# TensorE's blocks without a loop, two steps of attention moved into the block before, and w2 loaded later

## The chip, the cores and the metric

The kernel runs on one core of one Trainium2 chip. The metric is the device time in microseconds (us) of one execution; three runs of the kernel before are given, and one profiled execution. In the profile PE is TensorE's matmuls, PEld its weight loads, DVE VectorE, ACT ScalarE, POOL GpSimd and SP the engine that issues most DMAs; a q behind a name (SPq) is that engine's instruction queue.

## What is computed

A layer of a vision transformer over 32 images of 3 x 96 x 96, cut to 36 patches each: 1152 tokens of width 192. The token step, one attention layer with 12 heads of 64, and one layer of 8 experts of which each token uses one:

```python
out = jnp.einsum('rbnp,rep->bne', y, W_proj) + b_proj.sum(axis=0)      # tokens h
qkv = layernorm(h) @ W_qkv.T
logits = jnp.einsum('bhtd,bhsd->bhts', q, k) / SCALE                   # SCALE = 1/8
att = jax.nn.softmax(logits, axis=-1)
h = h + cat(att @ v) @ W_out.T
expert_idx = jnp.argmax(softmax(xt @ gate_w + gate_b), axis=-1)        # xt = layernorm(h)
for e in range(8):                                                     # gelu exact
    y = gelu(xt @ w1[e] + b1[e]) @ w2[e] + b2[e]
    out = jnp.where((expert_idx == e)[:, None], y, out)
h = h + out
```

## The kernel before, in words

The tokens are worked in NB = 4 blocks of BT = 288 tokens, each of NT = 3 row tiles of 96 tokens, and for attention in NU = 4 groups of two images (72 tokens). Each engine has its own program; semaphores join them. An opening does block 0's tokens, heads and values and the first scores. Then `body(b)` runs four times on TensorE, ScalarE, VectorE and GpSimd: three times in a hardware loop (`Fori(0, NB - 1)`, lines 670, 888, 1171, 1319) and once, shorter, for the last block (`last`). Since block b + 1's heads and values are computed in body b, a body holds: block b's attention, block b + 1's tokens, block b's output projection, norm and gate, and then block b + 1's q, k, v and scores 0 to 2. After the last body the tokens are ranked and gathered by expert and 16 tiles of 128 tokens run through the experts.

Attention of a group g takes these steps: `scores(g)` (TensorE, L465), `soften(g)` (VectorE, L994 and L995: subtract the maximum, frees the scores' banks by `sc_free`), `exponentials(g)` (ScalarE, L802), `normalise(g)` (VectorE, L1003 to L1005), `turn_probs(g)` (TensorE, L480, a transpose by 24 small matmuls, traced as 48), `take_probs(g)` (ScalarE, L816), `attend(g)` (TensorE, L495, product with v), `take_attended(g)` (ScalarE, L822). `turn_probs(g)` waits for the `take_probs` of the group before; `attend(g)` in the first place waits for `sc_free` of soften(3), since it writes the scores' banks.

Products into the four accumulator banks go through `product(key, b)`: the position of a key in `MIDDLE` (or `OPENING`, `FINAL`) modulo 4 gives its bank, so a product waits (`into`) until the one four keys before it has been taken out. In `MIDDLE` the keys from 6 are o0, o1, QK[0], QK[1], gt0, QK[2], o2, QK[3], QK[4], gt1, QK[5], QK[6], QK[7], gt2: ("o", 2) is number 12 and QK[5] number 16.

Around the row tiles: `project(t)` (TensorE, L506) gives a row tile of the attention's output, `take_o(t)` (VectorE, L1080) adds the residual, frees the bank and takes the statistics, `inverse_std` (GpSimd, L1290 and L1293) gives the inverse root, `finish_row(t)` (VectorE, L952) the normed row, `turn_rows(t)` (TensorE, L426) its transpose.

In each of the three loop bodies a third of w1 is split for the experts: `round_w1(b, 1)` on ScalarE (L786) copies w1B_part, `split_w1(b, 2)` and `split_w1(b, 3)` on VectorE (L1017) wait for it, `round_w1(b, 2)` (L788) copies the rest. In the body `split_w1(b, 2)` stands behind `take_o(2)` and `split_w1(b, 3)` last, behind `rank_tokens`.

SP's queue issues, in order: the first loads, the x of the following blocks, the normed rows of a block to the table in DRAM (`send_rows`), and for the last part w2 (4608 KB, into the memory of w_qkv, behind the last product with v of block 2's body), the rows of block 2, b2, half of b1 when the last attend is done (into the memory of v), the last rows, the other half of b1. TensorE waits for w2 (`w2_here`) before the experts, VectorE for b2 before `take_x` and for b1 before `add_b1`. GpSimd gathers the token rows from the table when all rows are sent and `ids` is there.

## Time and profile before

| | us |
|---|---|
| median of 3 runs | 319.29 |
| the runs | 319.29, 323.86, 317.44 |
| profiled execution | 320.99 |
| its span | 319.2 |
| PE / PEld busy | 270.7 / 246.5 |
| DVE / ACT / POOL busy | 171.2 / 130.1 / 64.1 |
| mean granted clock of TensorE | 0.918 |

The span is the time from the first to the last instruction; the rest of the profiled execution's 320.99 lies around it. Busy times of PE are those of pipelined matmuls. The program moves 28.12 MB at a mean of 88 GB/s. By the chain of work that ended last, TensorE holds 70% of the span, VectorE 11%, time in which an engine waited for nothing that the profile shows ("issue") 10%, ScalarE 5%.

### The profile page before, as it was taken

What the parts mean: (1) busy time and instruction counts of PE and PEld (TensorE: products, weight loads), DVE (VectorE), ACT (ScalarE), POOL (GpSimd) and SP (SyncE); (2) the same over time, 40 slices, a digit from 0 to 9 for tenths busy, and PEclk for the clock granted to TensorE, in tenths of its full rate; (3) what the DMA queues carried; (4) which work ended last, traced back from release to release, by engine and by line L of the source; (5) the groups of instructions that cost most, each with busy time, mean ns of one, the idle gap of its engine ahead of it and who ended that gap; (6) DMA issues with size and microseconds to landing.
All of it is one profiled execution on the core that took longest, in us unless ns stands there. A gap on an engine that the chain in (4) does not pass through costs nothing.

```text
span 319.2 us, 9680 instructions
## 1 busy us (share of the span) xinstructions
PE 270.7 (85%) x3710; PEld 246.5 (77%) x3711; DVE 171.2 (54%) x491; ACT 130.1 (41%) x354; POOL 64.1 (20%) x102
## 2 busy tenths in 40 slices
PE   7948989998999989499989747867479999999981
PEld 7928879897889987389988646747459998988871
DVE  7974286443787536836535840137146755655530
ACT  3463545535458364535454621220025344344220
POOL 2540002031003310002310000010602334334221
PEclk9987999799999999869999955695899999999997
DMA  7988600301001110000000393645300222121100
GB/s 258 267 321 326 265 3 4 113 3 55 3 0 28 83 55 0 6 4 2 4 0 2 113 422 118 191 149 212 99 26 13 63 74 49 55 68 34 31 3 0
DMA packets 6174, 28.12 MB, mean 88 GB/s; under 512 B 1495, under 2 KB 2787, under 8 KB 4990
## 3 DMA queue, kind: packets, MB, share of 16 engines
q1 hardware_dynamic: 4350, 23.62, 20.9%
q0 software_dynamic: 1792, 4.04, 4.7%
q8 instruction: 25, 0.41, 0.5%
q14 instruction: 7, 0.06, 0.1%
HBM read 24.99 MB, written 3.34 MB: 89 GB/s over the span
## 4 chain that ended last, share of the span: by engine, by line
PE 70%; DVE 11%; issue 10%; ACT 5%; POOL 1%; DVEq 1%; POOLq 0%; ACTq 0%
PE psum L433 22%; PE psum L714 10%; PE psum L506 9%; PE psum L418 5%; PE psum L480 4%; PE psum L495 4%; PE psum L542 4%; PE psum L702 3%; ACT w1B_part L786 2%; DVE total L1003 2%; PE psum L465 2%; PE psum L566 1%; DVE top L994 1%; DVE kT L995 1%; PE psum L426 1%
## 5 line engine op out<-in xcount | busy, mean ns | idle before, releaser
L1290 POOL TENSOR_SCALAR veps<-mv 96x1 f32<-96x1 f32 x24 | 8.2, 341 | 164.3 <-DVE mv L948 164.1
L433 PE MATMUL psum<-xn_hi,wq_parts 128*128 128x288 f32 x144 | 36.1, 320 | 4.0 <-DVE late_r L968 2.9
L714 PE MATMUL psum<-w2s,kT 128*128 x192 | 34.7, 331 | 2.8 <-issue 1.4
L714 PEld LDWEIGHTS psum<-w2s,kT 128*128 128x128 f32 x192 | 30.8, 190 | 4.8 <-issue 4.7
L506 PE MATMUL psum<-wo,oT 128*96 128x192 f32 x144 | 31.0, 376 | 0.7 <-ACT oT L822 0.7
L480 PE MATMUL psum<-ident,kT 36*36 36x36 f32 x768 | 18.8, 209 | 12.8 <-issue 7.7
L433 PEld LDWEIGHTS psum<-xn_hi,wq_parts 128*128 128x128 f32 x144 | 25.6, 197 | 5.0 <-issue 3.2
L480 PEld LDWEIGHTS psum<-ident,kT 36*36 36x36 f32 x768 | 16.8, 125 | 16.1 <-issue 15.3
L506 PEld LDWEIGHTS psum<-wo,oT 128*96 128x96 f32 x144 | 27.0, 193 | 2.3 <-issue 0.9
L433 PE MATMUL psum<-wq_parts,xn_hi 128*100 128x384 f32 x96 | 28.4, 350 | 0.0
L433 PE MATMUL psum<-late_r,wq_parts 128*128 128x288 f32 x96 | 28.4, 303 | 0.0
L1341 POOL DMA_INDIRECT out<-oT,ids x16 | 16.1, 1007 | 53.4 <-DVE oT L1229 53.4
L908 ACT ACTIVATE qT<-qT 128x512 f32<-128x512 f32 (+1 forms) x32 | 15.0, 515 | 25.3 <-DVE qT L1215 25.3
L433 PE MATMUL psum<-wq_parts,late_r 128*100 128x384 f32 x64 | 21.4, 335 | 0.0
L810 ACT COPY late<-psum 100x384 f32<-100x384 f32 x32 | 14.9, 476 | 15.8 <-PE psum L433 15.8
L1215 DVE TENSOR_TENSOR qT<-psum,late 128x512 f32<-128x512 f32 (+1 forms) x32 | 16.4, 553 | 8.3 <-PE psum L433 8.3
L418 PE MATMUL psum<-late,xb 128*96 128x192 f32 x108 | 20.0, 341 | 0.0
L1204 DVE TENSOR_TENSOR fx_lo<-psum,xn_hi 128x128 fp32r<-128x128 f32 x16 | 4.7, 292 | 27.4 <-issue 16.5
L1330 POOL DMA_INDIRECT xb<-token_table,ids x16 | 15.8, 985 | 16.9 <-DVE ids L1193 11.8
L433 PEld LDWEIGHTS psum<-late_r,wq_parts 128*128 128x128 f32 x96 | 18.9, 197 | 0.0
L418 PEld LDWEIGHTS psum<-late,xb 128*96 128x96 f32 x108 | 17.8, 170 | 0.5
L495 PE MATMUL psum<-late 36*64 36x36 f32 x768 | 17.4, 238 | 0.5 <-issue 0.4
(151 smaller groups left out, 573.2 us busy)
## 6 DMA issues: line engine op xcount, KB each, us to landing
w2s<-w SPq DMA_DIRECT2D x1, 4608.0 KB, 14.7
xb<-xT SPq DMA_DIRECT2D x4, 864.0 KB, 4.8
w1A_in<-w SPq DMA_DIRECT2D x3, 1024.0 KB, 7.5
w1B_in<-w SPq DMA_DIRECT2D x3, 1024.0 KB, 9.6
late<-b SPq DMA_DIRECT2D x2, 1536.0 KB, 7.4
token_table<-rows SPq DMA_DIRECT2D x4, 432.0 KB, 4.0
late<-w_proj SPq DMA_DIRECT2D x1, 960.0 KB, 4.9
kT<-b SPq DMA_DIRECT2D x1, 768.0 KB, 4.1
```

The source lines that it names most:

```text
L418: mm = pe.matmul(dst[0:TT, 0:D], xb[:, k, t * TT:(t + 1) * TT], weff[:, k // 2, k % 2, :], start=(k == 0), stop=(k == KX - 1))
L433: mm = pe.matmul(dst, lhsT, rhs, start=(i == 0), stop=(i == len(parts) - 1))
L480: mm = pe.matmul(psum[image, TR_BANK, cols], probs[image, g, cols], ident[image, image], start=True, stop=True)
L495: mm = pe.matmul(psum[DH * k:DH * (k + 1), SIDE_BANKS[i], at:at + PER_IMAGE], v[image, g, col:col + DH], probsT[image, g % 2, j * PER_IMAG ...
L506: mm = pe.matmul(dst[0:TT, 0:D], oT[:, c, t * TT:(t + 1) * TT], wo[:, c, :], start=(c == 0), stop=(c == PAIRS - 1))
L542: pe.transpose(psum[:, bank, 0:P], ident[:, :], ident[:, :])
L714: mm = pe.matmul(psum[:, 6, 0:D], hidT[i % 2][:, c * P:(c + 1) * P], w2s[:, bass.ds(e, 1), c, :], start=(c == 0), stop=(c == FCH - 1))
L810: act.copy(v[0:SPAN, g, f * (HD // 2):(f + 1) * (HD // 2)], acc(slot[0])[0:SPAN, 0:HD // 2]).then_inc(free[slot[0]], 1)
L908: ge = act.activation(hid[i % 2][:, lo:hi], hid[i % 2][:, lo:hi], ACT.Gelu)
L1215: dve.tensor_tensor(hid[i % 2][:, lo:hi], psum[:, 2 * (i % 2) + k, 0:hi - lo], b1s[:, bass.ds(e, 1), lo:hi].rearrange("p o f -> p (o f)"), ...
L1330: pool.indirect_dma_start(out=xg[j % 4], out_offset=None, in_=table, in_offset=bass.IndirectOffsetOnAxis(ap=ids[:, j:j + 1], axis=0)).then ...
L1341: pool.indirect_dma_start(out=out, out_offset=bass.IndirectOffsetOnAxis(ap=ids[:, j:j + 1], axis=0), in_=yo[j % 4], in_offset=None, bounds ...
```

## The change

TensorE's three bodies are written out, with a Python loop in place of `Fori`; the other engines keep theirs. The semaphore increments `passed("pe", pe)` go. `turn_probs(0)` and `scores(3)` of a block, which stood at its body's head, now stand in the tail of the body before (or of the opening), on TensorE around `ranks`; with them go `take_probs(0)` and `exponentials(3)` on ScalarE and `normalise(2)` and `soften(3)` on VectorE. `normalise(3)` becomes the first step of VectorE's body. `split_w1(b, 2)` moves ahead of `take_o(2)` and `split_w1(b, 3)` behind it, ahead of `finish_row(2)`. On SP's queue w2, b2 and the whole of b1 are issued one after another when the last attend is done; the rows of the last block are sent from ScalarE's queue, between `take_rows(1)` and `take_rows(2)`.

```diff
@@ sync
-                if b == NB - 2:
-                    complete(sp, product(VALUES[-1], b))
-                    sp.dma_start(w2s[:, :, :, :], w2).then_inc(w2_here, 16)
                 send_rows(b)
-            sp.wait_ge(tr_full, NU * NB)
+            sp.wait_ge(av_full, NU * NB)
+            sp.dma_start(w2s[:, :, :, :], w2).then_inc(w2_here, 16)
             sp.dma_start(b2s, b2.partition_broadcast(P)).then_inc(b2_here, 16)
-
-            sp.wait_ge(av_full, NU * NB)
-            sp.dma_start(b1s[:, 0:EXPERTS // 2, :], b1[0:EXPERTS // 2].partition_broadcast(P)).then_inc(b1_here, 16)
-            send_rows(NB - 1)
-            sp.dma_start(b1s[:, EXPERTS // 2:, :], b1[EXPERTS // 2:].partition_broadcast(P)).then_inc(b1_here, 16)
+            sp.dma_start(b1s, b1.partition_broadcast(P)).then_inc(b1_here, 16)
@@ tensor: scores, turn_probs and attend each lose passed("pe", pe); then the opening
-                if n in (0, 2, 4):
+                if n in (0, 2, 4, 7):
                     if n == 0:
                         all_taken(pe, QK, 0, opening=True)
-                    scores(n // 2, 0)
+                    scores({0: 0, 2: 1, 4: 2, 7: 3}[n], 0)
+                if n == 6:
+                    turn_probs(0, 0)
@@ tensor: body
-                attend_first()
                 if last:
+                    turn_probs(1, b)
                     pe.wait_ge(sc_free, NU * b + 5)
-                    attend_next(0)
+                    attend(0, b)
                     attend_next(1)
...
                 tokens(1, product(("tok", 1), b))
+                turn_probs(1, b)
                 pe.wait_ge(sc_free, NU * b + 5)
-                attend_next(0)
+                attend(0, b)
...
                 next_values((2, 1), (3, 0))
+                turn_probs(0, b + 1)
                 ranks(b)
                 next_values((3, 1))
+                scores(3, b + 1)
...
-            with pe.Fori(0, NB - 1) as b:
+            for b in range(NB - 1):
                 body(b, False)
@@ scalar
+            take_probs(0, 0)
+            exponentials(3, 0)
...
-                take_probs(0, b)
-                exponentials(3, b)
...
                     take_rows(1)
+                    act.wait_ge(rows_ready, NT * b + NT + 1)
+                    act.dma_start(table[b * BT:(b + 1) * BT, :].rearrange("(t p) d -> p t d", p=TT),
+                                  rows[:, :, :]).then_inc(rows_sent, 16)
                     take_rows(2)
...
-                next_values((3, 0), (3, 1))
+                next_values((3, 0))
+                take_probs(0, b + 1)
+                next_values((3, 1))
+                exponentials(3, b + 1)
                 round_w1(b, 2)
@@ vector
-            for g in range(3):
+            for g in range(NU):
                 soften(g, 0)
-                if g < 2:
+                if g < NU - 1:
                     normalise(g, 0)
...
-                normalise(2, b)
-                soften(3, b)
+                normalise(3, b)
                 if last:
-                    normalise(3, b)
...
                 take_tokens(0, product(("tok", 0), b))
-                normalise(3, b)
                 take_tokens(1, product(("tok", 1), b))
...
                 finish_row(1)
+                split_w1(b, 2)
                 take_o(2)
-                split_w1(b, 2)
+                split_w1(b, 3)
                 finish_row(2)
...
                 soften(2, b + 1)
+                normalise(2, b + 1)
+                soften(3, b + 1)
                 rank_tokens()
-                split_w1(b, 3)
...
-            dve.wait_ge(b1_here, 32)
+            dve.wait_ge(b1_here, 16)
```

## Rows read from the trace of the kernel before

**Rows 1.** Windows cut at TensorE's blocks 0, 1, 2 and the last attention.

```profile
core 0: us, PE busy (x) PEld busy (x) DVE busy (x) ACT busy (x) POOL busy (x), PEclk, DMA share, GB/s
45.13:88.91 43.78, 42.04 (x783) 38.44 (x782) 24.53 (x78) 21.89 (x62) 6.33 (x13) 0.96 0.10 33
88.91:131.16 42.25, 40.24 (x782) 36.94 (x781) 27.20 (x87) 23.41 (x63) 6.33 (x13) 1.00 0.10 32
131.16:180.15 48.99, 42.43 (x783) 38.85 (x782) 27.25 (x87) 23.55 (x63) 6.33 (x13) 0.93 0.01 3
180.15:195.50 15.35, 7.56 (x290) 7.16 (x289) 6.69 (x17) 5.74 (x9) 0.00 (x0) 0.66 0.87 338
```

**Rows 2.** Timeline of TensorE, head of block 2 (start, us, ..., idle before).

```profile
133.21 0.23 PE L480 MATMUL psum<-ident,kT 36*36 36x36 f32 x2 [2.05 <-issue]
136.47 1.48 PE L480 MATMUL psum<-ident,kT 36*36 36x36 f32 x43 [3.03 <-issue]
...
138.71 5.11 PE L418 MATMUL psum<-late,xb 128*96 128x192 f32 x24
```

**Rows 3.** DMA queue of instructions (packets, MB, share): block 1, then block 2.

```profile
q8 instruction: 2, 0.03, 0.4%
...
q8 instruction: 8, 0.13, 1.2%
```

**Rows 4.** Timelines of PE, ACT, DVE, POOL in the middle of block 1.

```profile
113.44 0.38 PE L433 MATMUL psum<-xn_hi,wq_parts 128*128 128x288 f32 x1
...
115.40 0.40 PE L433 MATMUL psum<-xn_hi,wq_parts 128*128 128x288 f32 x1 [0.38 <-ACT qT L792]
...
116.83 0.27 PE L426 MATMUL psum<-ident,rows 96*128 96x96 f32 x1 [0.50 <-DVE rows L952]
...
113.15 1.90 ACT L786 CAST w1B_part<-w1B_in 64x2048 fp32r x1
...
112.18 0.35 DVE L1080 TENSOR_TENSOR rows<-psum,hres 96x192 f32<-96x192 f32 x1 [1.23 <-PE psum L506]
...
115.17 1.22 DVE L1017 TENSOR_TENSOR w1B<-w1B_in,w1B_part 64x1024 f32 x1 [1.92 <-ACT w1B_part L786]
...
113.75 0.56 POOL L1293 TENSOR_TENSOR rstd<-veps,minus_half 96x1 f32<-96x1 f32 x1
```

**Rows 5.** Timeline of TensorE, turn 1 near the head of block 1.

```profile
95.12 0.96 PE L480 MATMUL psum<-ident,kT 36*36 36x36 f32 x45 [0.66 <-DVE kT L995]
```

**Rows 6.** Timelines: a projection in block 1; the last attention; ScalarE there.

```profile
102.93 2.12 PE L506 MATMUL psum<-wo,oT 128*96 128x192 f32 x12
...
181.00 0.87 PE L465 MATMUL psum<-kT,qT 64*36 64x36 f32 x46
186.26 1.56 PE L480 MATMUL psum<-ident,kT 36*36 36x36 f32 x45 [4.39 <-DVE kT L995]
...
192.65 0.76 PE L480 MATMUL psum<-ident,kT 36*36 36x36 f32 x18 [2.65 <-issue]
...
195.50 3.76 PE L506 MATMUL psum<-wo,oT 128*96 128x192 f32 x12 [0.74 <-ACT oT L822]
...
180.86 1.90 ACT L788 CAST w1B<-w1B_in  x1
```

**Rows 7.** An issue of SP; DMA issues (KB each, median us to landing); stores of rows (min/median/max).

```profile
204.09 0.33 SPq L402 DMA_DIRECT2D late<-b  x1
...
w2s<-w SPq DMA_DIRECT2D x1, 4608.0 KB, 14.7
late<-b SPq DMA_DIRECT2D x2, 1536.0 KB, 7.4
xb<-token_table,ids POOLq DMA_INDIRECT x16, 3.2
...
DMA to landing us min/median/max: 3.2/4.0/15.5
```

**Rows 8.** Timelines of GpSimd and VectorE: first gather, first product with b1 added.

```profile
224.55 1.24 POOL L1330 DMA_INDIRECT xb<-token_table,ids  x1 [11.80 <-DVE ids L1193]
...
235.15 1.02 DVE L1215 TENSOR_TENSOR qT<-psum,late 128x512 f32<-128x512 f32 x2
```

More of the change, by code:

```diff
@@ L283, in build @@
         pool_step = sem("pool_step")
-        waited = {"pe": sem("pe_waited"), "dve": sem("dve_waited"), "pool": sem("pool_waited")}
+        waited = {"dve": sem("dve_waited"), "pool": sem("pool_waited")}
         ident_ready = sem("ident_ready")
@@ L458, in scores @@
                 pe.wait_ge(sc_free, NU * b + g + 1)
-                passed("pe", pe)
                 for c in range(PAIRS):
@@ L474, in turn_probs @@
                 pe.wait_ge(tr_free, NU * b + g + 1)
-                passed("pe", pe)
                 for j in range(HEADS):
@@ L487, in attend @@
                 pe.wait_ge(av_free, NU * b + g + 1)
-                passed("pe", pe)
                 for c in range(PAIRS):
@@ L600, in products @@
                         heads(*key, product(key, b))
-                def attend_first():
-                    turn_probs(0, b)
-                    scores(3, b)
                 def attend_next(g):
```

## The prediction

> **What bounds the kernel now.** I read the windows first, cut at the starts of TensorE's blocks. In the first three blocks TensorE is busy for 42.04 of 43.78, 40.24 of 42.25 and 42.43 of 48.99 us [rows 1]: there TensorE is the path, and only its waits can be won. The reader is to see that blocks 0, 1 and 2 issue the same 782 or 783 matmuls and that block 2 is 48.99 − 42.25 = 6.74 us longer than block 1. Then the last attention: from 180.15 to 195.5 TensorE is busy for only 7.56 of 15.35 us at a granted clock of 0.66 [rows 1]. The timeline of TensorE says where: two stalls of 2.05 and 3.03 us at the head of block 2, released by nothing the profile shows [rows 2]; a wait of 4.39 us in the last block and, with w2 in flight, another stall of 2.65 us without a releaser [rows 6]. Last I read which instruction-queue packets ran: 2 in block 1, 8 in block 2 [rows 3].
>
> **The change, part by part.** Sums are in us against the profiled execution (span 319.2 in a run of 320.99); that run is 1.7 above the median of 319.29, and I carry the difference over to the median.
>
> *Loop written out (D).* Block 1 fetched almost nothing: its code was there from block 0. Block 2 fetched 8 packets and stood for 5.1 us at its first turn [rows 2, 3]; the rest of its 6.74 is the slow clock after it. Straight code reads on without a jump, so block 2 should cost what block 1 costs: −6.74. The price of no loop is that blocks 1 and 2 fetch all their code (E). Block 0 did so in straight order and took 43.78 at clock 0.96 against block 1's 42.25 at 1.00, a difference of 1.53 [rows 1]. Low end 0, high end 1.53 for block 1 and as much for block 2 again, 3.1. Block 2 after its stall streamed without another stall, so I take 0.5.
> The Trainium skill (Runtime: NRT & Kernel Launch, Instruction fetch mechanics) says that prefetch is purely sequential, that crossing a block of code is mostly hidden, and that a taken branch out of the resident window stalls. The trace agrees for the second jump (5.1 us) and not for the first, which shows no stall. By the page E would be 0 and the total 0.5 lower.
>
> *Turn 0 and scores 3 in the tail (C).* The same instructions run in almost the same order, so TensorE's own work is worth 0. What goes is the wait for soften(3) ahead of turn 1 in a middle block, 0.66 [rows 5]. But normalise(3) now stands ahead of take_tokens(0) on VectorE, behind rank_tokens, so the statistics of token tile 0 come about 1 us later and turn_tokens(0) waits for them. I take half: −0.3 at two boundaries, −0.6 (ends −1.3 and +0.6).
>
> *split_w1 moved around take_o(2) (A, B).* This part costs. In block 1, take_o(2) ran at 112.18. The product that begins at 113.44 (QK[5]) writes the accumulator bank that o2 used: key 12 and key 16 of MIDDLE, four banks. It therefore waits for take_o(2). Now split_w1(b, 2) stands ahead of take_o(2), and this split waits for ScalarE's w1B_part, a copy from 113.15 to 115.05: the split runs from 115.17 for 1.22 us [rows 4]. take_o(2) then starts at 116.31 and ends at 116.66, QK[5] starts at about 116.8 instead of 113.44: TensorE stands 3.3 us. Next late: the third row. From the start of take_o(2) to the end of its inverse root were 114.31 − 112.18 = 2.1 us [rows 4], now to 118.4; split 3 (1.22) behind the statistics ends at 118.6; finish_row(2) gives its transpose at about 119.0, against 116.83. QK[5] to QK[7] end at 118.8, so the end of this place moves by 119.0 − 116.83 = 2.15; the old waits of 0.38 and 0.50 are in it. Three blocks: +6.45 (A). The clock: after a gap of 5.1 us TensorE came back slow, twenty-four token matmuls after it included [rows 2]; after small waits it did not. A gap of 3.3 lies between. If the clock falls, QK[5] to QK[7] (2.05) take twice as long, less the 0.2 of slack, and what follows loses a little: 0 to 2 a block. I take 0.7, +2.1 for three (B). What split 3 gives back behind rank_tokens (1.22 on VectorE) is already in C. The twelve semaphore increments that go from TensorE's queue in each block I cost at 0: queued matmuls hide them; all the idle time of block 1 is 42.25 − 40.24 = 2.0 us [rows 1], and the waits named here (0.66, 0.38, 0.50) fill most of it.
>
> *The last attention (F).* Before, scores(3) ends at 181.87 and project(0) starts at 195.50, 13.6 later [rows 6]. Now soften(3) is done about 1.4 after scores(3); turn 1 fills the time; attend(0) ends at 2.2. Turn 2 needs take_probs(1), which is queued on ScalarE behind exponentials(3) (to 2.0) and round_w1(b, 2) (1.90 [rows 6]), so it ends at 4.4. Then turn 2 and attend(1) (0.9 + 0.8), copy out of attended (0.6), project(0) at 6.9; at half clock 7.7. Win 6.7 or 5.9; if the clock stays full, project(0) takes 2.12 instead of 3.76 [rows 6] and the win is 8.3. The stall of 2.65 beside w2 is inside this: w2 no longer flies then. I take −6.2 (ends −8.3 and −5.3). From project(0) on the chain of projections, norms, gate and ranks is as before.
>
> *w2, b2 and b1 behind the last attend; rows on ScalarE's queue (G).* Call A the end of the last attend (204.0 before, where SP issued the first half of b1 [rows 7]). w2 took 14.7 to land, half of b1 7.4 [rows 7]. In series, w2 at A+14.8, b2 (half the bytes of that b1 half, 3 to 4) at about A+18, b1 whole at A+26 to A+33 by these latencies, and at A+25 if they pipeline at w2's rate (4.7 MB in 14.7 us against 8.65 MB). TensorE needs w2 at about A+20; the first gather leaves at A+20.5, VectorE needs b1 at 235.15, A+31.2 [rows 8]. So w2 is covered by 5 us, b1 by 6 when pipelined, by nothing if serial at 33 (+2). But the first gathers now run beside b1, and TensorE waits for the first: 3.2 alone [rows 7]. The last rows are stored at A+9, now beside w2: such a store took 3.2 to 15.5 to land, the 15.5 queued behind w2 [rows 7]; landing at A+24.5 would hold the gathers by 4. Range 0 to 4.3; nearest row is the gather itself, half as long again: I take +1.5. The issue on ScalarE (about 0.3, as SP's) hides under TensorE's transpose of the third row. rows(2) no longer queue behind w2; nobody waited for them.
> The Trainium skill (DMA: Bandwidth & Descriptors, Queues, rings and completion order) says that a DMA engine takes turns packet by packet between the queue rows with work, and that SP and ScalarE own a row each. By that the last rows would not stand behind w2 and G is at its low end; by a single line it would be 4.3. No row of this trace has two such queues loaded.
>
> **Sum.** A 6.45 + B 2.1 + C −0.6 + D −6.74 + E 0.5 + F −6.2 + G 1.5 = −3.0. 319.3 − 3.0 = **316.3 us**, 0.9% less. About 2% (6.4 us) is what a measurement of this kernel can tell from no change: the three runs shown lie 317.44 to 323.86. So: no difference that counts.
>
> **Rivals.**
> 1. *The clock holds.* B = 0, project(0) at full clock (F −8.3), fetch free, G half: 6.45 − 0.6 − 6.74 − 8.3 + 0.7 = −8.5, **310.8**. For it: 0.66 and 0.38 of idle left the clock up. Against: the last attention keeps gaps of over 2 us and ran at 0.66. Chance 0.24.
> 2. *The gathers start late.* G = 4.3, rest as forecast: **319.1**. For it: 8.65 MB behind one another until A+25. Against: separate queues. Chance 0.12.
> 3. *Slower: straight code is fetched late.* Place: heads of code blocks while x or rows move, in blocks 1 and 2. Price of one late fetch: 2.65 as beside w2 [rows 6] and 1.7 of slow clock, 4.35. Three of them give −3.0 − 0.5 + 13.05 = +9.6, **328.9**; over 2% slower from the third on. For it: TensorE's two kinds of unexplained stall both came with fetches. Against: block 0 and the rest of block 2 streamed with at most 1.53 lost. Chance 0.07.
> 4. *The change does not do what it says:* the stall at block 2's head is no matter of the loop and returns. D = 0: **323.0**. For it: the first jump had no stall. Against: 8 packets against 2. Chance 0.07.
> Forecast: 0.50, its own range 313 to 320.
>
> **How the numbers follow.** Faster by over 2% (under 312.9): four fifths of rival 1 and 0.04 of the forecast, 0.23. Slower (over 325.7): rival 3 and a little of 4, 0.09. Within: 0.68. Range 310.5 to 322: it leaves out rival 3, half of rival 4 and the far end of rival 1.
>
> **What would show it.** D: no gap over 1 us at a block's head, block 2 within 1.5 of block 1. A: a wait of about 3.3 us of a QK product on VectorE's take_o(2) in each of three blocks, and turn_rows(2) waiting for finish_row(2). B: granted clock below 1.00 behind it. C: the 0.66 gone, perhaps a wait of turn_tokens(0). F: project(0) of the last block 7 to 8 us behind scores(3). G: first gather over 3.2 us, no wait of TensorE on w2. The forecast is wrong if QK[5] does not wait (then −9 or more), if w2 or b1 lands after its need, or if fetch stalls spread.

## The result, and the profile after

| | before | after |
|---|---|---|
| median, us | 318.49 (4 runs) | 327.07 (4 runs) |
| all runs, us | 317.44, 317.68, 319.29, 323.86 | 326.83, 326.88, 327.27, 330.33 |
| span of the profiled execution, us | 319.2 | 325.1 |
| granted clock of TensorE | 0.918 | 0.91 |

Some executions of this kernel fall in a slower state; all ratios leave them out, while the medians are over all executions. The ratio is 1.0305, with a 95% interval of 1.0215 to 1.0395: slower by 3%, where 316.3 us and "no difference that counts" were forecast. 327.07 lies 5 us above the upper end of the range, 322.

The page of the changed kernel, part 5 (group | busy, mean ns | idle before, what ended most of it) and part 4 (shares of the chain that ended last), already shows two of the causes:

```profile
PE 69%; DVE 9%; issue 6%; DMA 6%; ACT 5%; POOL 2%; DVEq 1%; POOLq 0%; ACTq 0%
...
L427 PE MATMUL psum<-xn_hi,wq_parts 128*128 128x288 f32 x144 | 40.1, 347 | 12.0 <-DVE rows L1078 9.2
...
L1327 POOL DMA_INDIRECT xb<-token_table,ids x16 | 15.7, 984 | 22.5 <-DMA token_table<-rows 17.1
```

The products with q and k now wait 9.2 us in all for `take_o` (L1078), three times 3.06. The gathers wait for the store of the last rows, and 6% of the chain is a DMA; before, the first gather followed `ids` on VectorE [rows 8].

To find where the time went, I cut both traces at the same four events of TensorE: the start of each block's token products, the end of the last block's fourth scores, and the start of its first output projection. Windows of after, then the same cuts in before (columns as in [rows 1]):

```profile
core 0: us, PE busy (x) PEld busy (x) DVE busy (x) ACT busy (x) POOL busy (x), PEclk, DMA share, GB/s
46.47:94.00 47.53, 43.55 (x788) 39.80 (x782) 25.49 (x75) 22.52 (x63) 7.17 (x13) 0.93 0.10 31
94.00:144.80 50.80, 46.20 (x788) 41.94 (x782) 27.41 (x86) 23.70 (x63) 7.16 (x13) 0.87 0.09 28
144.80:190.74 45.94, 41.72 (x796) 38.32 (x792) 27.40 (x86) 23.52 (x63) 7.17 (x13) 0.96 0.04 12
190.74:198.88 8.14, 4.72 (x193) 4.41 (x188) 4.78 (x17) 4.43 (x6) 0.00 (x0) 0.76 0.01 2
```

```profile
46.55:90.32 43.77, 42.03 (x787) 38.43 (x781) 24.68 (x81) 22.18 (x62) 6.33 (x13) 0.96 0.10 33
90.32:138.71 48.39, 41.30 (x789) 37.89 (x781) 30.18 (x93) 25.05 (x64) 6.33 (x13) 0.95 0.09 29
138.71:181.87 43.16, 41.66 (x784) 38.03 (x781) 24.51 (x80) 22.23 (x61) 6.33 (x13) 0.98 0.05 13
181.87:195.50 13.63, 5.85 (x193) 5.67 (x193) 5.37 (x11) 4.04 (x7) 0.00 (x0) 0.62 0.86 348
```

The three blocks are 3.8, 2.4 and 2.8 us longer, although the second no longer holds the loop's stall of 5.1 us [rows 2]. The last attention is 5.5 us shorter, a little less than the 5.9 to 6.7 of the forecast.

Each of the three blocks holds this place. Timelines of TensorE, VectorE and GpSimd in block 0 of after, and windows around it:

```profile
71.09 0.25 PE L420 MATMUL psum<-ident,rows 96*128 96x96 f32 x1
71.17 0.24 PE L421 MATMUL psum<-ident,rows 96*64 96x96 f32 x1
74.48 0.40 PE L427 MATMUL psum<-xn_hi,wq_parts 128*128 128x288 f32 x1 [3.06 <-DVE rows L1078]
...
76.05 0.44 PE L427 MATMUL psum<-late_r,wq_parts 128*128 128x288 f32 x1
...
72.94 1.22 DVE L1015 TENSOR_TENSOR w1B<-w1B_in,w1B_part 64x1024 f32 x1 [4.22 <-ACT w1B_part L778]
74.08 0.34 DVE L1078 TENSOR_TENSOR rows<-psum,hres 96x192 f32<-96x192 f32 x1
...
75.08 1.22 DVE L1015 TENSOR_TENSOR w1B<-w1B_in,w1B_part 64x1024 f32 x1
...
75.34 1.04 POOL L1287 TENSOR_SCALAR veps<-mv 96x1 f32<-96x1 f32 x1 [7.04 <-DVE mv L946]
```

```profile
73.00:75.50 2.50, 1.02 (x7) 1.02 (x8) 2.32 (x5) 0.42 (x4) 0.16 (x1) 0.99 0.00 0
75.50:78.50 3.00, 3.00 (x15) 2.78 (x14) 1.17 (x2) 1.47 (x5) 2.10 (x3) 0.50 0.05 16
```

VectorE is idle for 4.22 us in front of the split, which waits for ScalarE's copy of w1B_part; `take_o(2)` stands behind it, and TensorE's QK[5] behind that. After the gap the granted clock is 0.50 for 3 us, the lower of the two levels (1.2 of 2.4 GHz), and a product takes 0.44 instead of 0.30 us. In blocks 1 and 2 the same wait of 3.06 stands at 124.36 and 171.43.

At the other end, the last store and the first gather. Issues of ScalarE's queue and of GpSimd, TensorE's wait, and the DMA issues of 203 to 236 us (KB each, us to landing):

```profile
213.66 0.35 ACTq L854 DMA_DIRECT2D token_table<-rows  x1
...
230.36 1.24 POOL L1327 DMA_INDIRECT xb<-token_table,ids  x1 [17.14 <-DMA token_table<-rows]
...
w2s<-w SPq DMA_DIRECT2D x1, 4608.0 KB, 14.3
late<-b SPq DMA_DIRECT2D x1, 3072.0 KB, 22.9
kT<-b SPq DMA_DIRECT2D x1, 768.0 KB, 16.3
token_table<-rows ACTq DMA_DIRECT2D x1, 432.0 KB, 15.8
```

A store of 432 KB that had a queue to itself took 15.8 us, as long as the slowest store before, which stood behind w2 on one queue (15.5 [rows 7]). The first gather left at 230.36 instead of 224.55 [rows 8].

### The profile page after: what moved, and what is told of

Its sections match the earlier page's. It is cut to its first block, busy times and chain, and to the rows that moved or that the text cites. A ratio compares the mean times of both kernels' runs of the same rounds, so it can differ in the third digit from the quotient of the medians.

```text
span 325.1 us, 9601 instructions
## 1 busy us (share of the span) xinstructions
PE 273.1 (84%) x3710; PEld 247.9 (76%) x3711; DVE 171.5 (53%) x491; ACT 130.5 (40%) x354; POOL 66.6 (20%) x102
## 3 DMA queue, kind: packets, MB, share of 16 engines
q0 software_dynamic: 1792, 4.04, 4.5%
## 4 chain that ended last, share of the span: by engine, by line
PE 69%; DVE 9%; issue 6%; DMA 6%; ACT 5%; POOL 2%; DVEq 1%; POOLq 0%; ACTq 0%
PE psum L427 27%; PE psum L706 10%; PE psum L497 8%; DMA token_table<-rows 5%; PE psum L472 4%; PE psum L486 3%; PE psum L694 3%; PE psum L458 2%; PE psum L533 2%; PE psum L412 2%; ACT w1B_part L778 2%; PE psum L557 1%; DVE top L992 1%; DVE total L1001 1%; PE psum L420 1%
## 5 line engine op out<-in xcount | busy, mean ns | idle before, releaser
L427 PE MATMUL psum<-xn_hi,wq_parts 128*128 128x288 f32 x144 | 40.1, 347 | 12.0 <-DVE rows L1078 9.2
L1287 POOL TENSOR_SCALAR veps<-mv 96x1 f32<-96x1 f32 x24 | 10.7, 446 | 168.1 <-DVE mv L946 167.5
L427 PEld LDWEIGHTS psum<-xn_hi,wq_parts 128*128 128x128 f32 x144 | 29.1, 224 | 13.0 <-DVE rows L1078 9.8
L427 PE MATMUL psum<-late_r,wq_parts 128*128 128x288 f32 x96 | 31.1, 330 | 0.0
L497 PE MATMUL psum<-wo,oT 128*96 128x192 f32 x144 | 30.0, 366 | 0.7 <-ACT oT L814 0.7
L497 PEld LDWEIGHTS psum<-wo,oT 128*96 128x96 f32 x144 | 26.0, 187 | 2.0 <-issue 0.8
L1338 POOL DMA_INDIRECT out<-oT,ids x16 | 16.1, 1007 | 53.3 <-DVE oT L1226 53.3
L427 PEld LDWEIGHTS psum<-late_r,wq_parts 128*128 128x128 f32 x96 | 21.5, 224 | 0.0
L472 PEld LDWEIGHTS psum<-ident,kT 36*36 36x36 f32 x768 | 15.6, 120 | 5.7 <-issue 4.9
L472 PE MATMUL psum<-ident,kT 36*36 36x36 f32 x768 | 17.5, 204 | 2.6 <-ACT late L808 2.2
L784 ACT COPY qT<-psum 128x288 f32<-128x288 f32 x24 | 9.5, 398 | 23.0 <-PE psum L427 23.0
```

The lines of the kernel that those rows point to most:

```text
L427: mm = pe.matmul(dst, lhsT, rhs, start=(i == 0), stop=(i == len(parts) - 1))
L472: mm = pe.matmul(psum[image, TR_BANK, cols], probs[image, g, cols], ident[image, image], start=True, stop=True)
L497: mm = pe.matmul(dst[0:TT, 0:D], oT[:, c, t * TT:(t + 1) * TT], wo[:, c, :], start=(c == 0), stop=(c == PAIRS - 1))
L1287: pool.tensor_scalar(veps[:, kind, t:t + 1], mv[:, kind, t, 1:2], EPS, None, ALU.add).then_inc(pool_step, 1)
L1338: pool.indirect_dma_start(out=out, out_offset=bass.IndirectOffsetOnAxis(ap=ids[:, j:j + 1], axis=0), in_=yo[j % 4], in_offset=None, bounds ...
```

## The experiments

Each ratio is that to the kernel before, run on the same chip in the same batch.

### 1. The order of split_w1, undone and alone

```diff
# undo_split: the changed kernel with
+                take_o(2)
                 split_w1(b, 2)
-                take_o(2)
-                split_w1(b, 3)
                 finish_row(2)
...
                 rank_tokens()
+                split_w1(b, 3)
# split_only: the kernel before with the opposite edit
```

> The changed kernel, with split_w1(b, 2) and split_w1(b, 3) where they stood before (behind take_o(2), and behind rank_tokens). Theory: each of three blocks loses about 3.5 us because QK[5] waits for take_o(2), 2.2 of wait and 1.3 of slow clock behind it; so 327.1 - 10.5 = about 316.6 us, and no wait of TensorE on line L1078. Rival 1, the wait is covered by other work or taken back in the tail: 325 to 327. Rival 2, only the wait counts and the clock falls anyway: 320.5.

> The kernel before, with split_w1(b, 2) ahead of take_o(2) and split_w1(b, 3) ahead of finish_row(2), and nothing else changed. Theory: TensorE waits about 3.1 us for take_o(2) in each of three blocks and is slow behind it, +3.5 a block, about +10: 329. Rival, it costs only beside the other parts: under +4.

`undo_split`: 319.01 us, ratio 0.9956 (0.9908 to 1.0003), span 319.1. By the ratios that is 3.5% or 11 us under the changed kernel; the two medians, from different batches, are 8 us apart. Its block 0 took 43.90 against 47.53 us, 3.63 less, and around QK[5] only the two old waits of 0.38 and 0.49 us stand. From the start of block 0 to the end of the last scores(3) it took 181.31 − 46.47 = 134.84 against 144.27 us, 9.4 less. `split_only`: 332.44 us, ratio 1.0293 (1.0171 to 1.0414), with the wait of 3.06 us at 73.48, 129.90 and 175.82. Its ratio rests on two executions, and its trace also holds 1.4 us more of stalls without a releaser, up to the end of the last attention, than that of the kernel before, so not all of its 2.9% need be the order's. From both sides the order costs about 3%; this one part is as large as the whole loss.

### 2. The third row ahead of the second half of the split

```diff
                 take_o(2)
-                split_w1(b, 3)
                 finish_row(2)
+                split_w1(b, 3)
```

> The changed kernel with finish_row(2) ahead of split_w1(b, 3) instead of behind it. In the changed kernel GpSimd's first step of the third row took 1.04 us instead of 0.22 beside that split. Theory (the wait of 3.06 us of QK[5] for take_o(2) and the slow clock behind it are the whole cost, the third row is ready while TensorE still works through the slowed products): GpSimd's step is 0.22 again, the wait of 3.06 stays, the block's length stays within 0.3 us, 326 to 327 us. Rival (the third row sets the end of this place, as the sum of the prediction had it): 0.8 to 2 us less in each of three blocks, 321 to 324.5.

328.88 us, ratio 1.0145 (1.0084 to 1.0205), span 328.7. The interval doesn't meet that of the changed kernel, but the spans and the trace don't show this kernel to be faster: block 0 took 94.23 − 46.70 = 47.53 us, as in the changed kernel, the three blocks together 190.91 − 46.70 = 144.21 against 144.27, and the wait of 3.06 is there in each. The expected time (326 to 327) was missed by 2 us; another batch and another chip stand behind this one, with 323.76 for the kernel before. GpSimd's step, timeline of block 0:

```profile
75.65 0.22 POOL L1287 TENSOR_SCALAR veps<-mv 96x1 f32<-96x1 f32 x1 [7.03 <-DVE mv L946]
75.95 0.56 POOL L1290 TENSOR_TENSOR rstd<-veps,minus_half 96x1 f32<-96x1 f32 x1
77.10 1.49 POOL L1313 COPY hres<-h 96x576 f32<-96x576 f32 x1 [0.58 <-DVE rows L950]
```

So the step of 1.04 us is back at 0.22, and TensorE gains nothing: it is still busy with products at the lower clock when the row is ready. The product's own wait and the clock behind it are the cost, not the third row.

### 3. The loads and the last store, undone and alone

```diff
# undo_dma: the changed kernel with SP's queue of before (w2 from the last
# product with v of block 2 on, ahead of that block's rows; half of b1, the
# last rows, the other half); no store from ScalarE.
# undo_both: this and undo_split. dma_only: the kernel before with
+            sp.wait_ge(av_full, NU * NB)
+            sp.dma_start(w2s[:, :, :, :], w2).then_inc(w2_here, 16)
...
+                    act.dma_start(table[...], rows[:, :, :]).then_inc(rows_sent, 16)
```

> The changed kernel, with the loads of w2, b2 and b1 and the store of the last rows as before (w2 behind block 2's last product with v, rows on SP's queue between the halves of b1). Theory: the first gather no longer waits for the store of the last rows, -5.3 us; against that a stall of TensorE beside w2 in the last attention comes back, 2.65 us and slow clock, +0 to +5: 322 to 327. Rival, the late gather came from something else: it stays 5 us behind ids, 327 and more.

> The changed kernel with both the split order and the loads as before; what is left is TensorE without a loop and turn 0 and scores 3 in the tail. Theory: the two are independent and add: 327.1 - 10.5 - 5.3 + (0 to 5) = 311 to 316 us. If they do not add, the clock ties them together.

> The kernel before, with the loads of w2, b2 and b1 behind the last attend and the last rows stored from ScalarE's queue, nothing else changed. Theory: the store lands 15 us after its issue and the gathers wait 4 to 5 us for it; against that the stall of 2.65 beside w2 in the last attention goes, with some slow clock: +1 to +3, 320 to 322. Rival, the store is no slower than before: 315 to 316.

`undo_dma`: 329.33 us, ratio 1.0281 (1.0154 to 1.0409), span 329.2. `undo_both`: 318.97, 0.9937 (0.9882 to 0.9993), span 315.7. `dma_only`: 326.32, 1.016 (1.0075 to 1.0246), span 321.9. With the store of before, the gathers follow `ids` at once; but nothing is seen to be won, since a wait comes up elsewhere. VectorE in the last block of `undo_both`, then TensorE behind it:

```profile
187.27 0.61 DVE L1006 TENSOR_TENSOR kT<-kT,share 100x432 f32<-100x432 f32 x1
197.49 0.35 DVE L1081 TENSOR_TENSOR rows<-psum,hres 96x192 f32<-96x192 f32 x1 [9.61 <-DMA token_table<-rows]
...
200.18 0.39 PE L426 MATMUL psum<-ident,rows 96*128 96x96 f32 x1 [3.93 <-DVE rows L953]
```

`take_o(0)` of the last block overwrites the rows of block 2, whose store stands behind w2 on SP's queue. In the kernel before the last attention took 13.6 us and `take_o(0)` ran at 199.39, released by its projection; the store was out in time. Now that the attention takes 8.1, the store is late (in `undo_dma` the wait is 11.29, and 6.15 on TensorE). "Nobody waited for them", said the prediction; that held for before only. The stall of 2.65 us beside w2 was expected back here and didn't come: in `undo_dma`, `undo_both` and `rows_first` (experiment 8) w2 is in flight during the last attention and no such stall stands there, while `loop_back` has one of 2.10 us there with nothing of w2 in flight. So w2 was not its cause. And `dma_only` prices the changed DMA part by itself: its store took 16.1, its first gather left 17.44 us after GpSimd's last step, TensorE waited 7.27 us for it.

### 4. w2 and b1 in eight DMAs each

```diff
-            sp.dma_start(w2s[:, :, :, :], w2).then_inc(w2_here, 16)
+            for e in range(EXPERTS):
+                sp.dma_start(w2s[:, e:e + 1, :, :], w2[:, e:e + 1]).then_inc(w2_here, 16)
# b1 likewise; the waits count to 16 * EXPERTS
```

> The changed kernel, with w2 and b1 loaded in eight DMAs each (one expert each) at the same place and in the same order; the bytes are the same, a packet is an eighth (36 KB and 24 KB of one partition in one packet become 4.6 and 3 KB). Theory 1, a DMA engine takes turns between SP's and ScalarE's queues packet by packet: 19 packets of rows per engine stand each behind one large packet; with small ones the store lands in 4 to 6 us, not 15.8, and the time is 327.1 - 5.3 = about 321.8. Theory 2, a store waits for all bytes issued earlier, whatever the packets: it lands after 14 to 16 us and the time stays 327.

325.2 us, ratio 1.0183 (1.0091 to 1.0274), span 322.1. The last store landed after 8.6 instead of 15.8 us (the expectation said 4 to 6), and the gathers left at 225.20, right behind `ids`. Not all of that is won: now b1 is loaded beside the first gather, and from its issue to TensorE's first product 5.26 us pass instead of 3.36. 321.8 us had been expected. What a packet is, and who gets turns, the queues' rows show (packets, MB, share of 16 engines): in the changed kernel from 214 to 216 us, 218 to 220, 220 to 222, 224 to 226, then in `pieces` from 220 to 222.

```profile
q1 hardware_dynamic: 22, 0.81, 94.1%
...
q1 hardware_dynamic: 53, 0.63, 75.2%
q10 hardware_dynamic: 54, 0.08, 11.0%
...
q1 hardware_dynamic: 109, 0.68, 82.1%
q10 hardware_dynamic: 115, 0.18, 23.4%
...
q1 hardware_dynamic: 34, 0.84, 96.9%
q10 hardware_dynamic: 34, 0.05, 6.9%
```

```profile
q1 hardware_dynamic: 185, 0.56, 70.8%
q10 hardware_dynamic: 153, 0.21, 28.5%
```

q1 is SP's queue, q10 ScalarE's, which holds nothing but the 304 packets of the rows (0.44 MB, 1.4 KB each). It has no packet in the first 2 us, nor has it one in the first 3 us behind the issue in `pieces`. After that the counts of the two run side by side, 53 to 54, 109 to 115, 34 to 34: one turn each. But a packet of w2 is 0.81 MB / 22 = 37 KB, one of b1 0.84 / 34 = 25 KB, one of b2 6 KB. Beside b1 the rows get 7% of the engines, in the stretch where w2 ends and b2 begins 11%; beside b2 they get 23%, beside the smaller pieces 28%. The Trainium skill (DMA: Bandwidth & Descriptors, Queues, rings and completion order) says that a DMA engine takes turns packet by packet between queue rows, and the counts agree. It was my conclusion from it, "G is at its low end", that fell: a fair turn is no fair share when the packets differ eighteen to twenty-five fold.

### 5. The loop: written out alone, and put back

```diff
# unroll_only: the kernel before with
-            with pe.Fori(0, NB - 1) as b:
-                body(b, False)
+            for b in range(NB - 1):
+                body(b, False)
# loop_back: the changed kernel with the opposite edit and the passed("pe") of before
```

> The kernel before, with TensorE's three bodies written out and nothing else changed. Theory of the prediction: the 5.1 us at the head of block 2 go and the clock stays up behind it, -6.7; against it blocks 1 and 2 fetch their code, and beside the load of x in block 1 TensorE is late once and slows, as in block 0: +0 to +4. So 312 to 316 us where the kernel before takes 318.5. Rival, the stall is not the loop's: 318.5 and a gap at a block's head.

> The changed kernel with TensorE's loop back (and its semaphore increments at the waits); all else as changed. Theory: a stall of 3 to 5 us at the head of a block comes back, with slow clock behind it, and the late fetch of block 1 goes: +0 to +6 against the changed kernel. Rival, written out or not is the same to TensorE: within 1 us and a gap at the same place.

`unroll_only`: 315.78 us, ratio 0.986 (0.9788 to 0.9932), span 314.7. The stall at the head of block 2 is gone, as forecast, but not all of its 6.7 us is won: from the start of block 0 to the end of the last scores(3) it took 179.19 − 46.27 = 132.92 against 135.32 us before, 2.4 less. Block 1 took 136.94 − 90.12 = 46.82 us; from its start to the end of its first projection it lost 19.21 − 14.73 = 4.5. TensorE in it, then windows of it:

```profile
102.83 0.76 PE L480 MATMUL psum<-ident,kT 36*36 36x36 f32 x19 [1.09 <-issue]
105.29 4.04 PE L506 MATMUL psum<-wo,oT 128*96 128x192 f32 x12
...
104.00:109.50 5.50, 5.50 (x58) 4.53 (x56) 0.68 (x5) 1.72 (x8) 0.00 (x0) 0.50 0.20 81
```

A stall of 1.09 us that nothing in the profile released, and then 5.5 us at a granted clock of 0.50, in which a projection takes 4.04 instead of 2.12 us [rows 6]. `loop_back`: 333.02 us, ratio 1.0244 (1.0143 to 1.0345), span 327.3. Here the 5.1 us at the jump were expected back and didn't come: at the heads of blocks 1 and 2 it stood 0.38 and 0.31 us, with 0.79 in block 0 and 2.10 in the last attention. And `split_only`, whose code for TensorE is that of before, stalled at the first jump (2.55 and 2.60), not the second; `dma_only`, the same code again, at the second (1.71 and 2.75). So three kernels with the loop have a pair of stalls of 4.5 to 5.2 us at one jump, one has none, and no kernel without the loop has any. When it comes, and at which jump, is left open.

### 6. Is it the x load beside the fetch?

```diff
                 sp.wait_ge(xn_ready, NT * b)
+                if b >= 2:
+                    sp.wait_ge(rows_ready, NT * (b - 2) + 2)
                 sp.dma_start(xb[:, :, :], xT[b]).then_inc(x_here, 16)
# in undo_split
```

> The changed kernel with split_w1 in the order of before, and in which SyncE loads the x of the block after next only once the current block's row 0 is finished (some 20 us later, beside the products with q, k and v), and no longer during attend. Theory (the stall of 0.3 to 1.1 us before the turns of probabilities near 103 us in block 1, seen in every kernel with TensorE's blocks written out, comes from instruction packets fetched beside the x load, and the slow stretch behind it, project at 4.05 against 2.12 us, from the stall): no transfer then stands beside that fetch, the stall is gone, project is 2.12 in all blocks, blocks 0 to 2 together are 3 to 5 us shorter than without this edit, 314 to 316 us in all, ratio to before 0.98 to 0.985. Rival (the stall is the fetch's own and the slow clock comes of the wait of 1.5 us ahead of it, for turn_tokens(0)): stall and slow project stay, 319 us as without this edit. Second rival (the moved load meets another fetch): a stall of 1 to 3 us appears some 20 us later, beside the load.

318.43 us, ratio 1.005 (1.0003 to 1.0097), span 315.2. The DMA view of 96 to 108 us, then TensorE in that stretch:

```profile
q8 instruction: 2, 0.03, 1.2%
...
103.34 0.63 PE L474 MATMUL psum<-ident,kT 36*36 36x36 f32 x13 [0.60 <-issue]
105.62 4.04 PE L499 MATMUL psum<-wo,oT 128*96 128x192 f32 x12
```

Nothing moves but two packets of instructions, and the stall and the slow projection are still there. My theory fell: no other transfer is needed. Those two packets run at about 100.8 and 104.4 us and the stall from 102.74 to 103.34, between them: it begins 1.5 to 2.2 us behind a packet, as do the stalls in block 1 of the changed kernel, `undo_split`, `unroll_only` and `rows_first`. The expectation's rival, that the slow clock comes of the wait for `turn_tokens(0)` ahead of it (1.52 us in block 1), isn't enough alone either: block 2 has the same wait (1.53), no stall, and a first projection of 2.12.

### 7. The place of the code

```diff
+            for _ in range(64):            # 128, 192
+                passed("pe", pe)
# at the very start of TensorE's program, in the kernel rows_first of experiment 8
```

> The kernel with the four edits, and 64 semaphore increments at the very start of TensorE's program, where it waits for its first loads anyway: nothing is computed otherwise, only every later instruction of TensorE lies 64 places further in the code. Theory (block 1 stalls because a boundary between two fetched pieces of code falls into the dense stretch of small matmuls of its attention, and block 2 is spared because its boundaries lie elsewhere): the place or size of the stalls changes with the number of increments, 0.33 us and project(0) at 3.72 in block 1 become something else, with 64, 128 and 192 at least one kernel in which block 1 is within 0.7 us of block 2 (43 us) and one with a stall of over 0.5; times 308 to 314. Rival (the stall belongs to the block, not to the code's place): 0.3 to 0.9 us at the same instruction of block 1 in all three and none in block 2, 311.5 in each.

> The same with 128 increments. Theory: another place or size of the stalls than with 0, 64 and 192 increments, 308 to 314. Rival: as with 0, 311.5, the stall of block 1 at the same instruction.

> The same with 192 increments. Theory: another place or size of the stalls than with 0, 64 and 128 increments, 308 to 314. Rival: as with 0, 311.5, the stall of block 1 at the same instruction.

| increments | 0 | 64 | 128 | 192 |
|---|---|---|---|---|
| median, us | 311.52 | 319.14 | 330.11 | 340.73 |
| start of block 0, us | 46.69 | 55.32 | 65.36 | 75.82 |
| block 0, us | 44.19 | 41.62 | 41.62 | 42.42 |
| block 1, us | 44.86 | 45.82 | 43.26 | 43.16 |
| block 2 to its scores(3), us | 42.63 | 42.89 | 45.36 | 45.02 |
| the three | 131.68 | 130.33 | 130.24 | 130.60 |
| stall without a releaser ahead of the first projection, blocks 0, 1, 2 | 0.73, 0.33, none | none | none, 0.44, 0.77 | 0.60, 0.31, 0.48 |
| that projection, us | 3.71, 3.72, 2.12 | 2.12, 4.04, 2.33 | 2.12, 2.12, 3.61 | 2.12, 2.12, 3.61 |

Ratios: 0.9885 (0.9833 to 0.9937), 1.0219 (1.017 to 1.0268), 1.0536 (1.0447 to 1.0625). The column 0 is `rows_first`, from another batch (319.29 for the kernel before, here 323.76). Nothing of the computation differs, only where TensorE's instructions lie. The stalls move: without increments they stand in blocks 0 and 1, with 64 in none of the three, with 128 in blocks 1 and 2, with 192 in all three at other instructions. But the slow projection doesn't move with them. TensorE with 128, block 2, then with 64, block 1:

```profile
163.36 0.60 PE L492 MATMUL psum<-late 36*64 36x36 f32 x26 [0.77 <-issue]
164.27 3.61 PE L503 MATMUL psum<-wo,oT 128*96 128x192 f32 x12
...
105.71 0.27 PE L426 MATMUL psum<-ident,rows 96*128 96x96 f32 x1 [0.85 <-DVE rows L953]
107.98 1.47 PE L478 MATMUL psum<-ident,kT 36*36 36x36 f32 x45
111.10 4.04 PE L503 MATMUL psum<-wo,oT 128*96 128x192 f32 x12
```

So the stall follows the place of the code, and strikes in the dense run of small matmuls of attention. That it is a fetch that comes late is argued, from the moving and from the packet of instructions ahead of it; no packet runs while TensorE stands. The slow clock is another matter. With 64 increments TensorE's only idle time in block 1 before it is the wait of 0.85 us, and yet the granted clock falls to 0.50 from about 108.4 us on; in block 2 of `row_before_split` it is 0.50 from 155.0 to 160.9 with a wait of 0.79 as the only idle time. On the other side, stalls of 0.60 us (192 increments, block 0) and 0.70 (`rows_first_x`, block 0) left the projection at 2.12. So the clock can fall without a stall, and a stall of 0.70 doesn't always bring it down. What the clock costs by itself: with 64 increments block 1 took 18.20 us to the end of its first projection, with 128, a stall of 0.44 included, 15.66; the difference without that stall is 3.0 us. What makes it fall, no run here settles.

The Trainium skill (Runtime: NRT & Kernel Launch, Instruction fetch mechanics) calls the crossing from one block of code to the next mostly hidden; the trace agrees for most crossings (six or seven packets of the instruction queue a block, stalls of 0.2 to 1.1 us in one or two blocks of three, with 192 increments in all). The expected times (308 to 314) were wrong: I took the increments at the start for free, and each costs 0.15 us (below).

### 8. What the findings give together

```diff
# rows_first: the changed kernel with
                 take_o(2)
                 split_w1(b, 2)
                 finish_row(2)
+                split_w1(b, 3)
# and SP's end: rows of block 2, then
+            complete(sp, product(VALUES[-1], NB - 2))
+            sp.dma_start(w2s[:, :, :, :], w2).then_inc(w2_here, 16)
             sp.wait_ge(tr_full, NU * NB)
             sp.dma_start(b2s, b2.partition_broadcast(P)).then_inc(b2_here, 16)
             sp.wait_ge(av_full, NU * NB)
+            send_rows(NB - 1)
             sp.dma_start(b1s, b1.partition_broadcast(P)).then_inc(b1_here, 16)
# rows_first_x: with the later x load of experiment 6 as well
# no_tail: unroll_only with this end of SP's queue
```

> The changed kernel with four edits that the runs so far point to: take_o(2) ahead of both halves of the split (the first behind it, the second behind finish_row(2), where VectorE waits for the gate), rows of block 2 stored ahead of w2, w2 loaded from the last product with v of block 2 on (as before, not behind attend), and the last block's rows stored by SyncE ahead of b1. Theory: no wait of 3.06 us ahead of QK[5]; the last store takes 3 to 5 us instead of 15.8, so the gathers follow the ids at once and TensorE waits for the first one 2 us instead of 6.4 to 7.3; take_o(0) of the last block doesn't wait for block 2's store (9.6 us on VectorE in the kernel with both parts undone). 319.0 less 4.5 = 314.5, or 315.7 less the 3.9 us that TensorE waited for take_o(0) = 311.8: 311 to 315 us, ratio 0.965 to 0.985. Rival (w2 beside the last block's fetched code stalls TensorE as the loop's jump did): a stall of 2 to 3 us near 186 or later, 315 to 318.

> The kernel with the four edits and the later x load together. If both effects are real and apart: 3 to 5 us below the kernel with the four edits alone, 308 to 311 us, ratio 0.955 to 0.97. If the later x load does nothing: the same as that kernel.

> The kernel before with TensorE's blocks written out, block 2's rows stored ahead of w2 and b1 loaded whole behind the last rows: the first turn and the fourth scores stay at the head of each block. It prices the move into the tail by its difference to the kernel with the four edits. Theory (the move gives 5.5 us in the last attention, where nothing else fills TensorE, and costs 0.8 to 1.5 us a block at turn_tokens(0)): this kernel 2 to 4 us slower than the one with the four edits, 314 to 317. Rival (the move's costs in blocks 0 to 2 eat what it gives in the last): the same within 1 us, 312 to 314.

`rows_first`: 311.52 us, ratio 0.9838 (0.9763 to 0.9913), span 309.6: faster than both kernels. Its windows between the same four events, and the gather with TensorE's wait:

```profile
46.69:90.88 44.19, 42.20 (x789) 38.21 (x781) 25.48 (x75) 22.23 (x63) 7.16 (x13) 0.96 0.11 33
90.88:135.74 44.86, 42.44 (x789) 38.28 (x782) 27.36 (x86) 23.52 (x63) 7.17 (x13) 0.96 0.10 32
135.74:178.37 42.63, 40.58 (x795) 36.96 (x792) 27.38 (x86) 23.41 (x62) 7.16 (x13) 1.00 0.05 13
178.37:186.51 8.14, 4.71 (x193) 4.40 (x188) 4.78 (x17) 4.43 (x6) 0.00 (x0) 0.77 1.00 389
...
215.44 1.24 POOL L1328 DMA_INDIRECT xb<-token_table,ids  x1 [11.73 <-DVE ids L1191]
...
218.76 0.33 PE L676 MATMUL psum<-ident,xb 128*128 128x128 f32 x1 [1.99 <-DMA xb<-token_table,ids]
```

The last attention takes 8.14 us although w2 fills the DMA engines (share 1.00): moving w2 away was not needed for that. The four stores take 3.2 us in the median. Its gain over the kernel before is 1.6%, less than the 2% at which a difference counts here, but the interval lies wholly below 1. `rows_first_x`: 313.4, 0.9868 (0.9787 to 0.995), no gain, as experiment 6 says. `no_tail`: 315.45, 0.9902 (0.9855 to 0.9949), span 313.7. Its last attention takes 11.39 us, 3.25 more than with the tail moved, and the medians are 3.9 apart, in one batch. The two kernels also differ in the place of split_w1(b, 3) and in TensorE's increments, and their two intervals overlap; the last attention shows that the tail's move pays at the end, but how much of the 3.9 us is its own is not shown. The rival in which blocks 0 to 2 eat this up, the same time within 1 us, didn't come.

## Why the prediction was wrong, by its own steps

The ledger. The measured sizes come from the cuts above (before to after), for A and B from block 0 of `undo_split`, for E from `unroll_only`.

| term | forecast | measured |
|---|---|---|
| A + B, split ahead of take_o(2) | +8.5 | 3 x 3.63 = +10.9 |
| D, loop's stall | −6.7 | −6.7, taken over |
| E, straight code in blocks 0 to 2 | +0.5 | +4.3 |
| C, tail in blocks 0 to 2 | −0.6 | +0.4 |
| sum at the end of scores(3) | +1.7 | 190.74 − 181.87 = +8.9 |
| F, last attention to the experts' list | −6.2 | −8.4 |
| G, last store and first gather | +1.5 | +5.3 |
| sum | −3.0 | +5.8 (span +5.9) |

D is the forecast's own figure; only D + E is measured, −2.4 by `unroll_only`, which leaves +4.3 for E. C is what is left of +8.9 after the others, 8.9 − 10.9 + 6.7 − 4.3. In it stands what the order of split_w1 gives back: `turn_tokens(0)` waits 0.85 and 0.79 us in blocks 1 and 2, in `undo_split` 1.52 and 1.53, so that the order costs 9.4 in all and not 10.9.

**A and B: the mechanism right, the size short by 2.4.** The wait was forecast at 3.3 us in each of three blocks and is 3.06. The step that failed is the one after it: I let the third row set the end of this place and entered 2.15 (A) with 0.7 for the clock (B), within 0 to 2. In fact, the gap of TensorE counts nearly whole (3.06, less the old waits of 0.38 and 0.50), and the fifteen matmuls behind it run at a clock of 0.50 for 3 us, some 1.4 more; 3.06 − 0.88 + 1.4 = 3.6. Experiment 2 shows that the third row was not what set it.

**D right, and its price E, with G, the largest miss.** The stall at block 2's head is gone. But E was taken as 0.5 within 0 to 3.1, and block 1 alone cost 4.5 us more in `unroll_only`. The step that failed: I read the price from block 0's 1.53 us over block 1 without asking of what it consists. Block 0 of the kernel before holds a stall of 0.39 us without a releaser and a first projection of 3.54 instead of 2.12 us. In block 1 of `unroll_only` it is a stall of 1.09 and 5.5 us or more at a clock of 0.50, and the clock is the larger part. Rival 3 had a stall of 2.65 and 1.7 of slow clock for one place, 4.35; the size came, in one block, with the parts the other way round, and why the clock fell stays open (experiment 7). I gave rival 3 0.07 and three places. C missed by 1.0: the wait of `turn_tokens(0)` that it named is there (0.85 us in block 1, at 102.77).

**F right in its mechanism, its size in part luck.** 8.14 us from scores(3) to project(0), against 6.9 to 7.7 forecast, a win of 5.5 and not 5.9 to 6.7. What makes it −8.4 comes from behind project(0), where the forecast expected no change: there twenty-four matmuls of the projections took 4.14 us at full clock. In `undo_split` and `rows_first`, with the same last attention of 8.14 us, the same matmuls took 6.51 and 6.52.

**G: the wrong end of the range.** The bound of 4.3 stood there with its row, the store of 15.5 us [rows 7], and I took 1.5 since the store has its own queue. The step that failed is that reason; the packet counts of experiment 4 show why a queue of its own doesn't help. TensorE's first product of a gathered tile went from 227.93 to 233.72, 5.8 us, of which 0.5 came from earlier. That was rival 2, with 0.12. The rest of G held: TensorE never waited for w2, and b1 landed 24.4 us behind the last attend, where 25 was forecast (at w2's plain rate, 4.7 MB in 14.7 us, the 8.65 MB would have given 27).

**What tipped the sign.** Rival 2's delay and one place of rival 3's size came together, with B at its upper half: A + B 2.4, E 3.8, C 1.0, F −2.2 and G 3.8 make +8.8 over the forecast. I priced the rivals as cases apart; one late fetch or a late gather alone would have stayed inside 2%, and I gave no chance to them in one run, though nothing in the profile makes one exclude the other. That the split's place is the part that costs held: without that part the changed kernel is at 0.9956.

## What to carry to other kernels

Before moving an instruction ahead on an in-order engine, look at what it waits for: work that frees another engine's buffer must not stand behind a wait, and on TensorE, by the slower clock behind it, a gap of 3.06 us cost 3.6 beyond the 0.9 of waits that it replaced. A second DMA queue gave a small transfer one packet a turn, not half of the bandwidth; ahead of the large ones on the same queue the store took 3.3 us, and beside loads cut into small packets 8.6. Writing a loop out took a stall of 5.1 us away and brought back more than half of its worth in another block. When a tight chain gets shorter, ask which store or load was only just in time for the old length.

## What the hardware showed that I had not expected

- **VectorE and GpSimd in each other's way.** GpSimd's addition on 96 x 1 elements takes 0.22 us and took 1.04 to 1.05 beside VectorE's subtraction of two tiles in SBUF (1.22 us), in all three blocks (in the kernel before it already took 1.09 in another place of each of these blocks); with the order of experiment 2 it is 0.22 again, and the copy of `h` that now stands beside the subtraction goes from 0.66 to 1.49. The Trainium skill (SBUF — State Buffer, SBUF: two separate sides) describes a port pair that the two engines lock for a whole instruction; the trace agrees, GpSimd's step ends at 76.38 and the subtraction at 76.30.
- **A semaphore increment of TensorE's own is not free where nothing hides it.** The first matmul began at 1.80, 10.64, 20.41 and 30.19 us with 0, 64, 128 and 192 increments ahead of it: (30.19 − 10.64) / 128 = 0.153 us each. The change removes twelve a block; no run here prices those, where queued matmuls may cover them.
- **TensorE's clock can fall in a dense run of small matmuls without a gap of 1 us ahead of it.** With 64 increments block 1 has a wait of 0.85 us, no stall, and a projection of 4.04 instead of 2.12; in block 2 of the same kernel a wait of 0.79 is followed by one of 2.33, and with 128 increments a wait of 0.85 and a stall of 0.44 in block 1 by one of 2.12.
